# Order and engine of the weight splits in a linear-attention and mixture-of-experts kernel

## The chip, the cores and the metric

The kernel runs on one core of a Trainium2 chip. Its engines work side by side, each through its own list of instructions in order, and are tied together by semaphores: TensorE (PE), VectorE (DVE), ScalarE (ACT), GpSimd (POOL), and SyncE (SP), which issues most transfers. The metric is the device time in microseconds of one execution, as the median of several runs.

## What is computed

One transformer layer on 2048 tokens of width 512: `x = x + attention(layernorm(x))`, then `x = x + experts(layernorm(x))`. The reference, cut to what matters:

```python
# attention: 16 query heads, 4 key heads, width 128
q, k, v = x @ Wq.T, x @ Wk.T, x @ Wv.T          # q and k then rotated (rope)
qf, kf = elu(q) + 1.0, elu(k) + 1.0
def step(carry, inp):
    state, z = carry
    q_s, k_s, v_s = inp
    state = state + k_s[..., :, None] * v_s[..., None, :]
    z = z + k_s
    num = einsum('bhe,bhed->bhd', q_s, state)
    den = einsum('bhe,bhe->bh', q_s, z)[..., None] + EPS
    return ((state, z), num / den)
return out @ Wo.T
# experts: top 8 of 64 (32 real, 32 zero experts), gate, up and down projections
logits = xf @ w_cls.T
scores = softmax(logits)
act = silu(g) * u
y = einsum('eci,eih->ech', act, w_down)
```

## The kernel before

All data is float32. To keep precision on PE's faster float32 format, each operand is split in two: a high part, a copy rounded to that format (made on ACT), and a low part, the value minus its high part (a subtraction on DVE or POOL). A product is then three matmuls: high x high, high x low, low x high. Making high and low parts is most of what ACT, DVE and POOL do.

There are three blocks one behind the other, each closed by a barrier of all engines: `attention`, `routing` (projection by Wo, second layernorm, choice of experts, tables of slots) and `experts`. The change touches the first two.

`attention` goes over 16 chunks `c` of 128 tokens. A chunk has four groups `g` (one for each key head), and all engines loop over `n = 4 * c + g`. The loop is a software pipeline: PE projects group n, while rotation and feature map of n-1, the denominators of n-2, the transposes of n-3, the scores of n-4 and the output of n-5 are worked on. The order in which each engine takes them is written out by hand in its own loop. The 24 weight tiles of 128x512 (Wk, Wq, Wv) lie in `v_l` as loaded; `weight_high(i)` on ACT copies tile i to `w_h`, `weight_low(i)` on DVE writes `w_l`. PE's `project(u)` is a unit of twelve matmuls on four tiles; a chunk has six units, in the order k (0), q0 (1), q1 (2), v (3), q2 (4), q3 (5). In chunk 0 a unit also waits for its four low parts (line 206):

```python
if c == 0:
    eng.wait_ge(sm["wl"], 4 * i + 4)
```

So chunk 0 is where the splits and the pipeline's start share DVE and ACT. Before: ACT copies tiles 0 to 7 ahead of the loop, tiles 8 to 15 at n = 0 and 16 to 23 at n = 1, each batch at the head of its turn (lines 553 to 555). DVE makes tiles 8 to 11 at n = 0, 12 to 19 at n = 1 and 20 to 23 at n = 2, in a branch for chunk 0 that also holds the rotations (lines 433 to 444), ahead of `reduce` (denominators) and `feature_q` (which waits for ACT's `exps`).

Behind the last chunk the pipeline drains over n = 64 to 68. In its last three steps ACT and DVE also split tiles 0 to 5 of `wo` (`wo_high`, `wo_low`, lines 473 and 571), which lie in the same `v_l`, `w_h` and `w_l`. SP stores each group's output to `oT` in device memory (line 182) and loads the first three chunks of it again for routing (`load_o`).

`routing` also goes over 16 chunks. PE's `project(c, heads)` multiplies a chunk of oT by 16 tiles of Wo (one for each head, three matmuls each); in chunk 0 it waits for each head's `w_l` and for each quarter of `o_l` (lines 767 to 773). ACT (`high`, `o_high`) and DVE (`low`, `o_low`) split quarters 0 and 1 of o first, then tiles 6 and 7, quarter 2, tiles 8 and 9, quarter 3, and the tiles that are left. SP's `load(c)` brings the next chunk of oT and waits until it is stored.

## Time and profile before

| | us |
|---|---|
| median of 3 runs | 1025.86 |
| lowest and highest | 1021.43, 1032.84 |
| the profiled execution | 1021.43 |
| its span, first to last instruction | 1019.6 |
| attention block, about | 0 to 509 |
| routing block, about | 509 to 720 |

The profile holds one execution. The span leaves out 1.8 us around it. A row of a timeline begins with the start and the length of an instruction or of several of one kind in a row (xN), then engine, line of the program, operation, what it writes and reads; brackets at the end tell how long the engine had been idle and what released it. "PEclk" is the clock that TensorE was granted, 1.00 being 2.4 GHz and 0.50 being 1.2 GHz.

### The profile page before, as it was taken

What the parts mean: (1) busy time and instruction counts of PE and PEld (TensorE: products, weight loads), DVE (VectorE), ACT (ScalarE), POOL (GpSimd) and SP (SyncE); (2) the same over time, 40 slices, a digit from 0 to 9 for tenths busy, and PEclk for the clock granted to TensorE, in tenths of its full rate; (3) what the DMA queues carried; (4) which work ended last, traced back from release to release, by engine and by line L of the source; (5) the groups of instructions that cost most, each with busy time, mean ns of one, the idle gap of its engine ahead of it and who ended that gap; (6) DMA issues with size and microseconds to landing.
All of it is one profiled execution on the core that took longest, in us unless ns stands there. A gap on an engine that the chain in (4) does not pass through costs nothing. (4 is left out here: it accounts for less than half of the span.)

```text
span 1019.6 us, 14540 instructions
## 1 busy us (share of the span) xinstructions
PE 909.3 (89%) x4377; PEld 736.6 (72%) x4377; DVE 766.4 (75%) x1821; ACT 503.8 (49%) x867; POOL 494.5 (48%) x420
## 2 busy tenths in 40 slices
PE   4789999999999999999799999999759988697960
PEld 3577888888888888888578888888547666475850
DVE  6977988888888888888877777776577967586730
ACT  5454555555555555554652222222237867575730
POOL 2466766666667666666500000000046456667652
PEclk9999999999999999999999999999859999798995
DMA  8001111111111111112653653431149999898743
GB/s 296 6 32 47 58 37 58 47 58 42 51 54 46 48 48 58 42 48 86 262 193 133 257 194 127 142 136 65 64 149 286 330 287 269 227 276 262 216 64 41
DMA packets 52759, 131.03 MB, mean 129 GB/s; under 512 B 12156, under 2 KB 14588, under 8 KB 46528
## 3 DMA queue, kind: packets, MB, share of 16 engines
q1 hardware_dynamic: 41248, 114.67, 32.1%
q0 software_dynamic: 11424, 15.29, 8.3%
q8 instruction: 43, 0.70, 0.3%
q14 instruction: 44, 0.36, 0.1%
HBM read 106.53 MB, written 35.91 MB: 140 GB/s over the span
## 5 line engine op out<-in xcount | busy, mean ns | idle before, releaser
L595 POOL TENSOR_TENSOR a_t<-a_t 128x512 f32<-128x512 f32 x80 | 105.1, 1314 | 101.8 <-DVE a_t L358 101.8
L1076 DVE TENSOR_TENSOR w_l<-raw,w_h 128x1024 fp32r<-128x1024 f32 x96 | 114.8, 1222 | 13.4 <-ACT w_h L1069 11.7
L604 POOL TENSOR_TENSOR a_fQ<-a_fQ,a_den 128x512 f32<-128x512 f32 x64 | 88.0, 1376 | 71.8 <-DVE a_den L396 71.8
L213 PE MATMUL a_PQ<-w_h,a_xT_h 128*128 128x512 f32 x384 | 106.7, 400 | 10.3 <-DVE w_l L345 9.6
L775 PE MATMUL r_PY<-w_h,r_o_h 128*128 128x512 f32 x256 | 106.5, 416 | 3.4 <-DVE r_o_l L866 3.4
L1046 POOL TENSOR_SCALAR r_vr<-r_mv 128x1 f32<-128x1 f32 x16 | 8.4, 525 | 205.3 <-DVE r_mv L877 205.3
L1174 POOL DMA_INDIRECT out<-m_y,si x38 | 66.0, 1736 | 78.9 <-DMA out<-m_y,si 51.7
L213 PE MATMUL a_PQ<-w_l,a_xT_h 128*128 128x512 f32 x384 | 103.7, 392 | 0.0
L213 PE MATMUL a_PQ<-w_h,a_xT_l 128*128 128x512 f32 x384 | 103.5, 392 | 0.0
L775 PE MATMUL r_PY<-w_h,r_o_l 128*128 128x512 f32 x256 | 101.9, 398 | 0.0
L1069 ACT ACTIVATE w_h<-raw 128x1024 fp32r<-128x1024 f32 x96 | 97.8, 1054 | 8.1 <-DMA m_ident<-in_cr 7.8
L775 PE MATMUL r_PY<-w_l,r_o_h 128*128 128x512 f32 x256 | 101.7, 397 | 0.0
L392 DVE CUSTOM_DVE_ANT_0 a_m<-a_fQ,a_z 128x128 f32<-128x128 f32 x256 | 100.4, 445 | 0.0
L611 POOL TENSOR_TENSOR a_A_l<-a_A,a_A_h 128x512 fp32r<-128x512 f32 x64 | 89.0, 1390 | 6.5 <-ACT a_A_h L480 6.5
L213 PEld LDWEIGHTS a_PQ<-w_h,a_xT_h 128*128 128x128 f32 x384 | 70.2, 190 | 25.5 <-issue 11.4
L357 DVE TENSOR_TENSOR a_t<-a_PQ,a_tab 128x512 f32<-128x512 f32 x80 | 55.0, 688 | 42.0 <-PE a_PQ L213 42.0
L213 PEld LDWEIGHTS a_PQ<-w_l,a_xT_h 128*128 128x128 f32 x384 | 72.7, 189 | 15.7
L213 PEld LDWEIGHTS a_PQ<-w_h,a_xT_l 128*128 128x128 f32 x384 | 72.7, 189 | 15.3
L494 ACT ACTIVATE a_t<-a_t 128x512 f32<-128x512 f32 x80 | 50.0, 626 | 67.6 <-POOL a_t L595 67.6
L1155 POOL DMA_INDIRECT m_xg<-xn2d,si x58 | 71.9, 1239 | 19.9 <-issue 16.8
L480 ACT ACTIVATE a_QT_h<-a_PT 128x512 fp32r<-128x512 f32 x64 | 38.1, 596 | 80.9 <-PE a_PT L221 80.9
L775 PEld LDWEIGHTS r_PY<-w_h,r_o_h 128*128 128x128 f32 x256 | 48.7, 190 | 12.7 <-issue 3.8
(169 smaller groups left out, 2184.7 us busy)
## 6 DMA issues: line engine op xcount, KB each, us to landing
raw<-in_wgu SPq DMA_DIRECT2D x32, 1024.0 KB
oT<-a_o SPq DMA_DIRECT2D x64, 256.0 KB, 2.4
raw<-in_wd SPq DMA_DIRECT2D x32, 512.0 KB
...
```

The costliest lines, as they stand in the source:

```text
L213: last = eng.matmul(bank[:, :], a[:, k, :], w[:, 4 * i + k, :], start=s == 0 and k == 0, stop=s == 2 and k == 3)
L357: eng.tensor_tensor(heads(t1[:, r % 2, :]), q, spread(tab[:, c % 2, 0, :]), ALU.mult)
L392: last = eng.tensor_tensor_reduce(m[:, cols], fQ[:, n % 3, cols], z[:, c % 2, g * P:(g + 1) * P], 1.0, 1e-6, ALU.mult, ALU.add, den[:, n % ...
L494: eng.activation(t2[:, r % 2, :], t1[:, r % 2, :], ACT.Relu, scale=-1.0).then_inc(sm["r"], 1)
L595: eng.tensor_tensor(t1[:, r % 2, :], t1[:, r % 2, :], t2[:, r % 2, :], ALU.add).then_inc(sm["xr"], 1)
L604: eng.tensor_tensor(q, q, den[:, n % 2, :].unsqueeze(2).broadcast_to([P, 4, P]), ALU.mult).then_inc(sm["fs"], 1)
L611: eng.tensor_tensor(A_l[:, n % 2, :], A[:, n % 2, :], f(A_h[:, n % 2, :]), ALU.subtract).then_inc(sm["Al"], 1)
L775: last = eng.matmul(PY[c % 2][:, :], a[:, c % 2, h * P:(h + 1) * P], b[:, h, :], start=h == 0 and s == 0, stop=h == NH - 1 and s == 2)
L1069: eng.activation(high, src, ACT.Copy).then_inc(sm["m_wh"], 1)
L1076: eng.tensor_tensor(low, src, high.bitcast(F32), ALU.subtract).then_inc(sm["m_wl"], 1)
L1155: eng.indirect_dma_start(xg[:, e % 6, t, :], None, xn2d[:, :], bass.IndirectOffsetOnAxis(ap=ids[:, i:i + 1], axis=0), bounds_check=T - 1, ...
L1174: eng.indirect_dma_start(out[:, :], bass.IndirectOffsetOnAxis(ap=si[:, i:i + 1], axis=0), y[:, e % 4, t, :], None, compute_op=ALU.add).the ...
```

## The change

It changes three things. In chunk 0 of attention, ACT and DVE split four tiles at each of n = 0 to 3 (the tiles 4(g+2) to 4(g+2)+3). ACT does it at the head of each turn; DVE behind `reduce` and `feature_q` of the turn and, for n > 0, ahead of the rotation of q. The last tile of each four (11, 15, 19, 23) gets its low part on POOL, at the head of its turn, with a semaphore of its own (`wlp`), and PE waits for both. In the drain of attention, `wo_high` and `wo_low` are gone; all 16 tiles of Wo are split in routing: two tiles, then all of chunk 0 of o, then 14 tiles, and PE waits for the whole of `o_l` ahead of its first matmul. And SP waits at the end of attention until all of oT is stored, in place of routing's `load`.

```diff
+        def on_pool(i):
+            return i >= 11 and i % 4 == 3
...
                 load_o(2)
+                for b in range(2):
+                    eng.wait_ge(sm[f"oT{b}"], 16 * (NG // 2))
...
                     if c == 0:
-                        eng.wait_ge(sm["wl"], 4 * i + 4)
+                        eng.wait_ge(sm["wl"], 4 * i + 4 - max(i - 1, 0))
+                        if i >= 2:
+                            eng.wait_ge(sm["wlp"], i - 1)
...
                 for n in range(NG + 5):
                     c, g = divmod(n, 4)
-                    if c == 0:
-                        if g == 0:
-                            rotate(unit_k(0), rot_k(0), 0)
-                        if g == 2:
-                            v_low(0)
-                        for i in ((8,), (12,), (20,), ())[g]:
-                            for k in range(4):
-                                weight_low(i + k)
-                        rotate(unit_q(n), rot_q(n), 0)
-                        if g == 1:
-                            for k in range(4):
-                                weight_low(16 + k)
                     if 0 <= n - 2 < NG:
                         reduce(n - 2)
                     if 0 <= n - 1 < NG:
                         feature_q(n - 1)
                     if g == 2 and 1 <= c < NC:
                         s_low(c - 1)
-                    if g == 0 and 1 <= c < NC:
+                    if g == 0 and c < NC:
                         rotate(unit_k(c), rot_k(c), c)
-                    if g == 2 and 1 <= c < NC:
+                    if c == 0:
+                        for k in range(4):
+                            weight_low(4 * (g + 2) + k)
+                    if g == 2 and c < NC:
                         v_low(c)
-                    if 1 <= c < NC:
+                    if n < NG:
                         rotate(unit_q(n), rot_q(n), c)
...
-                    if n >= NG + 2:
-                        wo_low(2 * (n - NG - 2))
-                        wo_low(2 * (n - NG - 2) + 1)
...
-                    if n < 2:
-                        for i in range(8 + 8 * n, 16 + 8 * n):
-                            weight_high(i)
+                    if c == 0:
+                        for k in range(4):
+                            weight_high(4 * (g + 2) + k)
                     if 0 <= n - 1 < NG:
                         exps(rot_q(n - 1))
...
-                    if n >= NG + 2:
-                        wo_high(2 * (n - NG - 2))
-                        wo_high(2 * (n - NG - 2) + 1)
...
+                    if c == 0 and on_pool(4 * (g + 2) + 3):
+                        weight_low(4 * (g + 2) + 3)
                     if 0 <= n - 2 < NG:
                         scale(n - 2)
...
                 def load(c):
-                    eng.wait_ge(sm["r_ol"], 4 * (c - 2))
-                    for b in range(2):
-                        eng.wait_ge(sm[f"oT{b}"], 16 * (2 * c + 2))
+                    if c >= 3:
+                        eng.wait_ge(sm["r_ol"], 4 * (c - 2))
...
-                        if c >= 1:
-                            eng.wait_ge(sm["r_ol"], 4 * c + 4)
+                        eng.wait_ge(sm["r_ol"], 4 * c + 4)
...
                         if c == 0:
                             eng.wait_ge(sm["r_wol"], h + 1)
-                            eng.wait_ge(sm["r_ol"], h // 4 + 1)
```

ACT's list in chunk 0, before, from the high copies of tiles 8 to 11 to the first of q0's `exps` (`a_t` and `a_e` are the two activations of `exps`):

```order
L480 ACTIVATE w_h<-v_l 128x512 [waits e_st3]
L480 ACTIVATE w_h<-v_l 128x512 x3
L480 ACTIVATE w_h<-v_l 128x512 [waits e_st4]
L480 ACTIVATE w_h<-v_l 128x512 x3
L494 ACTIVATE a_t<-a_t 128x512 [waits e_xr]
L496 ACTIVATE a_e<-a_t 128x512 [waits e_r]
L480 ACTIVATE a_K_h<-a_fK 128x512 [waits e_f]
L480 ACTIVATE w_h<-v_l 128x512 [waits e_st5]
L480 ACTIVATE w_h<-v_l 128x512 x3
L480 ACTIVATE w_h<-v_l 128x512 [waits e_st6]
L480 ACTIVATE w_h<-v_l 128x512 x3
L494 ACTIVATE a_t<-a_t 128x512 [waits e_xr]
```

Only K's `exps` and high part stand among the copies. And now, from the high copies of tiles 12 to 15 on:

```order
L473 ACTIVATE w_h<-v_l 128x512 [waits e_st4]
L473 ACTIVATE w_h<-v_l 128x512 x3
L487 ACTIVATE a_t<-a_t 128x512 [waits e_xr]
L489 ACTIVATE a_e<-a_t 128x512 [waits e_r]
L473 ACTIVATE a_KT_h<-a_PT 128x512 [waits e_pt]
L473 ACTIVATE a_z<-a_PZ 128x512 [waits e_zc]
L473 ACTIVATE w_h<-v_l 128x512 [waits e_st5]
L473 ACTIVATE w_h<-v_l 128x512 x3
L487 ACTIVATE a_t<-a_t 128x512 [waits e_xr]
L489 ACTIVATE a_e<-a_t 128x512 [waits e_r]
L473 ACTIVATE a_V_h<-a_PQ 128x512 [waits e_pq]
L473 ACTIVATE a_xT_h<-a_PT 128x512 [waits e_pt]
L473 ACTIVATE w_h<-v_l 128x512 [waits e_st6]
```

The copies of tiles 12 to 15 (`e_st4`) stand behind K's exponentials and its high part, those of 16 to 19 (`e_st5`) behind q0's, and those of 20 to 23 (`e_st6`) behind the high part of the next x (`a_xT_h`).

DVE's list, before, from the low parts of tiles 12 to 15 to the low part of V:

```order
L345 TENSOR_TENSOR w_l<-v_l,w_h 128x512 [waits e_wh] x4
L357 TENSOR_TENSOR a_t<-a_PQ,a_tab 128x512 [waits e_f,e_pq]
L358 TENSOR_TENSOR a_t<-a_PQ,a_tab 128x512
L345 TENSOR_TENSOR w_l<-v_l,w_h 128x512 [waits e_wh] x4
L364 SCALAR_TENSOR_TENSOR a_fQ<-a_t,a_e 128x512 [waits e_e]
L401 TENSOR_TENSOR a_KT_l<-a_PT,a_KT_h 128x512 [waits e_th]
L333 TENSOR_SCALAR a_xn<-a_xin,a_mv,a_vr 128x512 [waits e_pt,e_rstd]
L379 TENSOR_TENSOR a_V_l<-a_PQ,a_V_h 128x512 [waits e_Vh]
```

Eight tiles and the rotation of q1 stand ahead of the first feature map of q. And now, from the low parts of tiles 8 to 10 to those of tiles 12 to 14 and the rotation of q1:

```order
L354 TENSOR_TENSOR w_l<-v_l,w_h 128x512 [waits e_wh] x3
L366 TENSOR_TENSOR a_t<-a_PQ,a_tab 128x512 [waits e_tab0,e_pq]
L367 TENSOR_TENSOR a_t<-a_PQ,a_tab 128x512
L373 SCALAR_TENSOR_TENSOR a_fK<-a_t,a_e 128x512 [waits e_e]
L332 BN_STATS a_st<-a_xin 128x6 [waits e_x1]
L334 BN_AGGR a_mv<-a_st 128x2 [waits e_bn]
L373 SCALAR_TENSOR_TENSOR a_fQ<-a_t,a_e 128x512 [waits e_e]
L354 TENSOR_TENSOR w_l<-v_l,w_h 128x512 [waits e_wh] x3
L366 TENSOR_TENSOR a_t<-a_PQ,a_tab 128x512 [waits e_f,e_pq]
L367 TENSOR_TENSOR a_t<-a_PQ,a_tab 128x512
```

The first feature map of q (`a_fQ`) stands now ahead of tiles 12 to 14; before, tiles 12 to 19 were ahead of it.

DVE's start of routing before, from the block's first operation on (`r_o_l` is the low part of a quarter of o, `w_l` of a tile of Wo):

```order
L937 MEMSET r_neg 128x1
L866 TENSOR_TENSOR r_o_l<-v_l,r_o_h 128x512 [waits e_r_oh] x2
L859 TENSOR_TENSOR w_l<-v_l,w_h 128x512 [waits e_r_woh] x2
L866 TENSOR_TENSOR r_o_l<-v_l,r_o_h 128x512 [waits e_r_oh]
L859 TENSOR_TENSOR w_l<-v_l,w_h 128x512 [waits e_r_woh] x2
L866 TENSOR_TENSOR r_o_l<-v_l,r_o_h 128x512 [waits e_r_oh]
L859 TENSOR_TENSOR w_l<-v_l,w_h 128x512 [waits e_r_woh] x6
```

Quarters of o and tiles of Wo took turns there. And now:

```order
L925 MEMSET r_neg 128x1
L847 TENSOR_TENSOR w_l<-v_l,w_h 128x512 [waits e_r_woh] x2
L854 TENSOR_TENSOR r_o_l<-v_l,r_o_h 128x512 [waits e_r_oh] x4
L847 TENSOR_TENSOR w_l<-v_l,w_h 128x512 [waits e_r_woh] x14
L933 CAST r_trib<-r_cst 128x128 [waits e_r_cst]
```

The four quarters now stand together behind two tiles, and 14 tiles follow.

## Rows read from the trace of the kernel before

**Rows 1.** The page: busy share of PE, and one group of POOL's instructions
```profile
PE 909.3 (89%) x4377; PEld 736.6 (72%) x4377; DVE 766.4 (75%) x1821; ACT 503.8 (49%) x867; POOL 494.5 (48%) x420
...
L595 POOL TENSOR_TENSOR a_t<-a_t 128x512 f32<-128x512 f32 x80 | 105.1, 1314 | 101.8 <-DVE a_t L358 101.8
```

**Rows 2.** Windows: stretch, us, busy PE, PEld, DVE, ACT, POOL, PEclk, DMA, GB/s
```profile
30.00:42.00 12.00, 8.44 (x40) 6.25 (x39) 11.97 (x26) 2.86 (x6) 3.25 (x3) 1.00 0.00 1
...
53.00:64.00 11.00, 8.33 (x37) 6.74 (x38) 10.04 (x29) 6.74 (x12) 7.82 (x8) 0.84 0.16 48
...
79.00:108.00 29.00, 27.37 (x130) 22.38 (x129) 22.52 (x57) 15.08 (x27) 18.05 (x16) 0.94 0.11 37
...
108.00:137.00 29.00, 29.00 (x147) 24.20 (x146) 24.89 (x66) 15.37 (x28) 19.12 (x17) 1.00 0.16 51
```

**Rows 3.** Waits of 0:50: who waited for whom, us, times, longest
```profile
PE a_PQ L213 <- DVE w_l L345: 9.6, 5, 3.4
```

**Rows 4.** Timeline of chunk 0 and the start of chunk 1
```profile
14.64 2.19 ACT L480 ACTIVATE w_h<-v_l 128x512 fp32r<-128x512 f32 x4 [0.84 <-DMA v_l<-in_wq]
...
18.14 3.58 DVE L345 TENSOR_TENSOR w_l<-v_l,w_h 128x512 fp32r<-128x512 f32 x4
...
18.30 1.66 POOL L595 TENSOR_TENSOR a_t<-a_t 128x512 f32<-128x512 f32 x1 [12.09 <-DVE a_t L358]
...
20.66 0.63 ACT L496 ACTIVATE a_e<-a_t 128x512 f32<-128x512 f32 x1
...
21.86 1.15 PE L213 MATMUL a_PQ<-w_h,a_xT_h 128*128 128x512 f32 x4 [2.20 <-DVE w_l L345]
...
23.76 1.08 PE L213 MATMUL a_PQ<-w_h,a_xT_l 128*128 128x512 f32 x4
...
28.24 1.17 PE L213 MATMUL a_PQ<-w_h,a_xT_h 128*128 128x512 f32 x4 [1.05 <-DVE w_l L345]
...
32.94 1.17 PE L213 MATMUL a_PQ<-w_h,a_xT_h 128*128 128x512 f32 x4 [1.70 <-DVE w_l L345]
...
36.42 0.60 ACT L480 ACTIVATE a_xT_h<-a_PT 128x512 fp32r<-128x512 f32 x1 [3.56 <-PE a_PT L221]
...
37.61 1.17 PE L213 MATMUL a_PQ<-w_h,a_xT_h 128*128 128x512 f32 x4 [1.22 <-DVE w_l L345]
...
42.20 1.09 PE L213 MATMUL a_PQ<-w_h,a_xT_h 128*128 128x512 f32 x4
...
46.48 0.29 DVE L392 CUSTOM_DVE_ANT_0 a_m<-a_fQ,a_z 128x128 f32<-128x128 f32 x1
...
57.29 0.50 PE L235 MATMUL a_PZ<-a_K_h,a_tri_r 128*128 128x512 f32 x1 [1.36 <-POOL a_K_l L599]
```

**Rows 5.** Timeline of the seam between attention and routing
```profile
500.78 1.14 ACT L480 ACTIVATE w_h<-v_l 128x512 fp32r<-128x512 f32 x2
...
503.32 0.68 DVE L414 TENSOR_TENSOR a_A<-a_PS,a_cst 128x512 f32<-128x512 f32 x1
...
507.92 0.60 ACT L480 ACTIVATE a_o<-a_PO 128x512 f32<-128x512 f32 x1 [0.69 <-PE a_PO L274]
...
508.96 0.38 SPq L162 DMA_DIRECT2D v_h<-oT  x1
...
509.76 1.15 ACT L989 ACTIVATE r_o_h<-v_l 128x512 fp32r<-128x512 f32 x2 [1.25 <-PEq L141]
...
511.26 0.47 PE L775 MATMUL r_PY<-w_h,r_o_h 128*128 128x512 f32 x1 [3.39 <-DVE r_o_l L866]
...
515.25 3.69 DVE L859 TENSOR_TENSOR w_l<-v_l,w_h 128x512 fp32r<-128x512 f32 x6
```

**Rows 6.** Windows with a low clock, columns as in rows 2
```profile
58.65:61.20 2.55, 2.55 (x11) 2.26 (x10) 2.55 (x5) 2.23 (x5) 2.55 (x3) 0.51 0.00 0
...
511.20:515.00 3.80, 3.74 (x10) 2.94 (x11) 3.80 (x7) 3.80 (x9) 0.00 (x0) 0.57 0.96 314
```

**Rows 7.** Tile a_o: its stores to oT, from issue to landing
```profile
DMA to landing us min/median/max: 2.3/2.4/5.3
```

More of the change, by code:

```diff
@@ L343, in weight_low @@
                 def weight_low(i):
+                    if on_pool(i):
+                        return
                     eng.wait_ge(sm["wh"], i + 1)
@@ L540, in out @@
                     copy(o[:, n % 2, :], PO[:, :], "o")
-                def wo_high(i):
-                    if i % 4 == 0:
-                        eng.wait_ge(sm[f"r_wo{i // 4}"], 16)
-                    copy(w_h[:, i, :], v_l[:, i, :], "r_woh")
                 weight_high(0)
@@ L591, in rstd, with weight_low @@
                     eng.tensor_tensor(vr[:, c % 2, 1:2], vr[:, c % 2, 0:1], neg[:, :], ALU.pow).then_inc(sm["rstd"], 1)
+                def weight_low(i):
+                    eng.wait_ge(sm["wh"], i + 1)
+                    eng.tensor_tensor(w_l[:, i, :], v_l[:, i, :], f(w_h[:, i, :]), ALU.subtract).then_inc(sm["wlp"], 1)
                 def add(u, r):
@@ L937, in _ @@
                 eng.memset(neg[:, :], -0.5).then_inc(sm["r_neg"], 1)
-                o_low(0, 0)
-                o_low(0, 1)
-                low(6)
-                low(7)
-                o_low(0, 2)
-                low(8)
-                low(9)
-                o_low(0, 3)
-                for i in range(10, NH):
+                low(0)
+                low(1)
+                for q in range(4):
+                    o_low(0, q)
+                for i in range(2, NH):
                     low(i)
@@ L994, in high, with o_high @@
                     copy(wo_h[:, i, :], v_l[:, i, :], "r_woh")
-                def o_high(c, quarters=range(4)):
+                def o_high(c):
                     if c >= NC:
@@ L1001, in o_high @@
                     eng.wait_ge(sm[f"r_o{c % 3}"], 16 * (c // 3 + 1))
-                    for q in quarters:
+                    for q in range(4):
                         rows, cols = quarter(c, q)
                         copy(heads(o_h[:, c % 2, cols]), rows, "r_oh")
-                o_high(0, (0, 1))
-                high(6)
-                high(7)
-                o_high(0, (2,))
-                high(8)
-                high(9)
-                o_high(0, (3,))
-                for i in range(10, NH):
+                high(0)
+                high(1)
+                o_high(0)
+                for i in range(2, NH):
                     high(i)
```

3 lines of the change are left out of this document (removed).

## Prediction

> **What bounds the kernel now.** First the page's busy line: TensorE (PE) is busy for 909.3 of 1019.6 us [rows 1]. Then the windows by stage: from 108 us on the attention loop keeps PE busy for 29.00 of 29.00 us at full clock, while 53:64 has 8.33 of 11 us with a granted clock of 0.84 and 79:108 has 27.37 of 29 with 0.94 [rows 2]. So a late start of the loop is not caught up later: PE has no slack to give. Then the waits of the first 50 us: PE waited 9.6 us, five times, for DVE's `w_l` [rows 3]; that is chunk 0, where the six weight blocks (units 0 to 5 of four 128-row tiles) are split while they are first used. Last the timelines of the two places that the change touches: chunk 0 [rows 4] and the seam between attention and routing [rows 5].
>
> **Part 1, chunk 0.** I follow the new order with the durations of before. Prices: four high copies on ACT take 2.19 us, the two activations of `exps` 0.63 each with a small gap, 1.3 together; four low parts on DVE take 3.58 beside a POOL operation; a unit on PE runs from 21.86 to 24.84, 2.98 [rows 4]; a POOL operation on 128x512 takes 1.31 [rows 1], up to 1.66 beside DVE's `w_l` [rows 4]. Without POOL six low parts take 3.69, 0.61 each [rows 5].
> Unit 2 (needs tiles 8 to 11). ACT is through tile 11 at 16.83, as before. POOL does tile 11 at 16.9 to 18.2, just ahead of the first rotation's addition, which started at 18.30 and still does. DVE does three tiles from 18.14: 2.9 in place of 3.58. Unit 2 starts at 21.2, 0.7 sooner than 21.86.
> Unit 3 (tiles 12 to 15). Before, ACT copied these high halves ahead of `exps(k)`, in time that it idled. Now they stand behind `k_high`, and `exps(q0)` behind them; and DVE has `feature_q(0)`, which needs `exps(q0)`, ahead of its low parts. So: `k_high` done 23.6, four copies 25.7, `exps(q0)` 27.0, `feature_q(0)` 27.7, three low parts at 0.61 and an end 29.5. Unit 3 starts at 29.6 against 28.24: +1.4.
> Unit 4 (16 to 19). The rotation of q1 (two operations at 0.6 apart and an end, 1.3) to 30.8; POOL's addition, behind its tile 15, to 32.2; `exps(q1)` 33.5; `feature_q(1)` 34.2; three low parts, partly beside POOL's tile 19 and its scaling, 36.3. Beside the same wait stand `turn_low_k`, `normal(1)` and `reduce(0)`, some 2.4 us of DVE in a wait of 2.8, which cost nothing. Unit 4 starts at 36.4 against 32.94: +3.5.
> Unit 5 (20 to 23) is the worst. Its high copies stand behind `xT_high(1)`, which waits for the transpose of the next x, and that stands on PE behind unit 4. Before, ACT had long made them and then idled 3.56 us before `xT_high(1)` at 36.42 [rows 4]. Now: unit 4 ends 39.4 (40.4 with the clock, below), transpose and `xT_high(1)` 41.7, four copies 43.9, `exps(q2)` 45.2, `feature_q(2)` 45.9, three low parts beside POOL 48.1. Unit 5 starts at 48.2 against 37.61: +10.6.
> The clock. After PE had done little from 54 to 58 us its granted clock was 0.51 over 58.65:61.20, and after the seam 0.57 over 511.20:515.00 [rows 6]: the 1.2 GHz level for about 2.5 and 3.7 us, half of which is lost. In the new order PE idles 3.9 us ahead of unit 4 and some 7 ahead of unit 5, so I add 1.0 to unit 4 (may or may not fall) and 2.1 to unit 5. The bounds are 0 and 2.5 for each, the upper the half of a fall of 5 us.
> Unit 5 then ends at 53.3, q0's transpose and `rest_k` about 1.1 later, and unit 6 starts at 54.4 against 42.20. That is +12.2 on PE, but before the delay passed on was DVE's: `reduce(2)` started at 46.48, 4.3 us after unit 6. Now rotation q3, `turn_low_q(0)` and `stats(2)` end at 56.0, so DVE is +9.5. The chain to `sum_k(1)` (57.29 before, after a wait for `K_l` [rows 4]) is DVE, ACT and POOL work of the same kinds; with fewer hold-ups in it I take +8.7 there. PE's stalls up to that point in before (much of the 2.67 idle us of 53:64) are swallowed. The low clock right behind, 1.25 us, is likely gone too, since PE now arrives there out of a busy stretch: +7.5. From there on the two kernels do the same in the same state, and I let the stalls of 79:108 return. Bounds of the start: +4 (no low clock and a cheaper chain) and +11 (5 us of it at both units).
>
> **A rule weighed.** Beside POOL's addition four low parts took 3.58 us, and with POOL idle six took 3.69 [rows 4, 5]. The Trainium skill's GPSIMD Engine Reference (Architecture) says that POOL shares its SBUF interfaces with VectorE and contends with its instructions that read two SBUF tensors; a low part is one. By that rule, and the trace agrees, a tile moved to POOL returns up to 1.1 us of the DVE time it saves if low parts run beside it. This is why I book almost no gain for the four moved tiles (0.7 on unit 2 alone). Were there no contention, DVE would gain 0.6 for each.
> The low clock after a quiet PE is the row's [rows 6]. The Trainium skill's TensorE: Matmul & The Clock Gate (Part 1) says that the array stands at half rate by default and activity releases it; by the rule unit 5 starts slow, as I have it, and without it the sum would be 2 to 3 us less.
>
> **Part 2, the seam.** Six of `wo`'s tiles are no longer split in the last three steps of attention. There two high copies stood ahead of the output copy at 500.78, two low parts (1.96 us) held `masked(63)` until 503.32, and two more copies of both kinds followed; the last output copy ran 507.92 to 508.52 [rows 5]. Without them the mask starts two low parts (1.2) sooner, at 502.1, and ends at 502.8; `A_h` 503.5, `A_l` on POOL 504.9, the last `attend` 506.1, output copy 506.7. That is 1.8 sooner.
> SP then waits for the stores of `oT` before the block ends. A store lands 2.4 us after its issue [rows 7]: 506.8 + 2.4 = 509.2, and 0.4 for the barrier (before, SP's last issue ended at 509.34 and ACT started at 509.76 [rows 5]) gives 509.6. All engines wait here, but the 1.8 pays for it: -0.1. Bounds: -1.3 (landing hidden) and +3 (the maximum of 5.3 [rows 7]).
> Then routing. Before, PE started 1.50 us after ACT, at 511.26, since six heads were ready and each quarter of o was waited for by itself. Now ACT does two high copies and four of `o_h`, 6 at 0.55 = 3.3, the last `o_low` ends 0.75 later, and PE starts 4.05 after ACT: +2.55. Behind it nothing falls short: a matmul takes 0.24 (eight between 21.86 and 23.76 [rows 4]), so a head takes PE 0.71 and its low part DVE 0.61. ACT and DVE have six tiles more before `o_high(1)` and `o_low(1)`, which end about 525.8, while PE comes to chunk 1 at 526.6: hidden by 0.8 us, and a later price if that cover goes. PE has been idle 7 us in place of 3.4, so 0.4 more of the low clock. `load(c)` loses only waits that are met, at no cost. Seam: -0.1 + 2.55 + 0.4 = +2.9.
> Experts are untouched.
>
> **Sum.** +7.5 + 2.9 = +10.4. The profiled execution took 1021.43, so 1031.8 for it; the median of the runs is 1025.86, 4.4 above it, so 1036.3 for a median.
>
> **Rivals.** (A) Not slower: DVE, and no order, bounds chunk 0. It is busy 11.97 of the 12 us of 30:42 [rows 2], and four low parts fewer save it 3.6. Then the start is -3.6, the seam +2.9, 1025.2. For it: that busy share. Against it: much of it is low parts done early, and the new order puts an ACT chain ahead of them. It decides at `feature_q(0)`: DVE must find `exps(q0)` done there, and ACT cannot have it before 27.0. (B) Given back: a fresh start also removes the stalls of 79:108 (1.6 idle and about 1.4 of clock [rows 2]): +7.4, 1033.3. For it: those stalls are remnants of a late DVE. Against it: `sum_k(1)` brings both kernels to the same state. (C) More clock and contention: low clock for 5 us at units 4 and 5 and behind `sum_k(1)` (+1.9 and +1.3) and the longer landing (+1): +14.6, 1040.5. Speaks for it: the idle stretches are longer than any of before.
>
> **How the numbers follow.** My forecast 0.48, A 0.10, B 0.25, C 0.17. The forecast's own range is 1032 to 1040. With the other cases the range is 1028 to 1042: A and the tail of C are left out. A measurement tells about 1% (10.3 us) from no change, that is 1036.1. C (0.17), half of my forecast (0.24) and a little of B (0.04) lie above: 0.45. Faster by over 1% would need more than A and gets 0.03; the rest, 0.52, lies within.
>
> **What would show it.** Right: unit 2 a little earlier, then PE waiting at units 3, 4, 5 with starts near 29.6, 36.4 and 48; ACT's copies of tiles 20 to 23 after `xT_high(1)`; full PE from about 115 on; the attention's last output copy 1.8 sooner relative to the loop, the barrier as late as before, PE's first routing matmul 4 us after ACT's. Wrong: `exps(q0)` ahead of 27 us, unit 5 before 44, or PE's idle of chunks 1 and 2 gone.

## The result, and the profile after

The changed kernel took 1045.31 us (median of 6 runs, 1041.33 to 1047.62), the kernel before on the same chip 1028.0 (6 runs, 1021.43 to 1032.84). The ratio is 1.0155, with a 95% interval of 1.0121 to 1.0190: slower by 12 to 20 us. This ratio, like those below, is the recorded one of fast runs and not the quotient of the two medians, which would be 1.0168 (all 20 runs of the changed kernel on record have a median of 1043.3). The forecast was +10.4, and its range of 1028 to 1042 does not hold 1045.31. The profiled execution took 1039.17, its span is 1037.4 with a mean granted clock of 0.943 (before 1019.6 and 0.957).

The page shows the same work (914.7 us of PE where [rows 1] has 909.3) and one large new wait:

```profile
PE 914.7 (88%) x4377; PEld 741.6 (71%) x4377; DVE 767.0 (74%) x1817; ACT 502.9 (48%) x867; POOL 496.6 (48%) x424
...
L220 PE MATMUL a_PQ<-w_h,a_xT_h 128*128 128x512 f32 x384 | 109.3, 407 | 21.8 <-DVE w_l L354 21.8
```

PE now waits 21.8 us for low parts where it waited 9.6 [rows 3]: the damage is in chunk 0. The windows (columns as in rows 2) say what kind of time it is:

```profile
30.00:42.00 12.00, 6.79 (x23) 5.14 (x22) 8.27 (x18) 1.75 (x3) 4.10 (x3) 0.72 0.00 1
53.00:64.00 11.00, 11.00 (x49) 8.97 (x49) 8.00 (x20) 2.18 (x4) 3.96 (x4) 0.90 0.04 12
37.80:42.30 4.50, 4.50 (x12) 3.55 (x13) 0.50 (x1) 0.00 (x0) 0.00 (x0) 0.59 0.00 0
50.40:56.30 5.90, 5.89 (x18) 4.73 (x19) 0.67 (x2) 0.23 (x1) 0.00 (x0) 0.60 0.01 3
91.00:120.00 29.00, 27.39 (x131) 22.38 (x130) 22.51 (x58) 15.97 (x28) 17.84 (x15) 0.94 0.12 41
120.00:149.00 29.00, 29.00 (x147) 24.22 (x146) 24.85 (x65) 15.35 (x29) 19.36 (x16) 1.00 0.15 46
527.20:531.00 3.80, 3.76 (x9) 2.99 (x10) 3.80 (x7) 3.80 (x8) 0.00 (x0) 0.50 0.80 283
```

First line: DVE, busy for 11.97 of these 12 us in before [rows 2], is busy for 8.27. Nothing is saturated there; the engines wait for each other. Lines 3 and 4 are units 4 and 5, both at about the 1.2 GHz level. Line 5 is the window 79:108 of [rows 2], 12 us later and with the same 27.4 busy us and the same clock of 0.94; from there on PE is full (line 6), but for one wait of 0.9 us between chunks 9 and 10. The timeline of chunk 0, against [rows 4]:

```profile
20.95 1.99 PE L220 MATMUL a_PQ<-w_h,a_xT_h 128*128 128x512 f32 x4 [2.66 <-DVE w_l L354]
25.95 0.63 ACT L489 ACTIVATE a_e<-a_t 128x512 f32<-128x512 f32 x1
26.61 1.06 DVE L373 SCALAR_TENSOR_TENSOR a_fQ<-a_t,a_e 128x512 f32<-128x512 f32 x1 [2.32 <-ACT a_e L489]
27.60 1.88 DVE L354 TENSOR_TENSOR w_l<-v_l,w_h 128x512 fp32r<-128x512 f32 x3
29.58 1.17 PE L220 MATMUL a_PQ<-w_h,a_xT_h 128*128 128x512 f32 x4 [3.15 <-DVE w_l L354]
30.76 1.29 POOL L584 TENSOR_TENSOR a_t<-a_t 128x512 f32<-128x512 f32 x1 [3.63 <-DVE a_t L367]
31.20 1.13 DVE L340 TENSOR_SCALAR a_xn<-a_xin,a_mv,a_vr 128x512 f32<-128x512 f32 x1
32.01 1.45 POOL L580 TENSOR_TENSOR w_l<-v_l,w_h 128x512 fp32r<-128x512 f32 x1
32.25 1.36 DVE L401 CUSTOM_DVE_ANT_0 a_m<-a_fQ,a_z 128x128 f32<-128x128 f32 x1
32.75 0.63 ACT L489 ACTIVATE a_e<-a_t 128x512 f32<-128x512 f32 x1
34.39 0.66 DVE L373 SCALAR_TENSOR_TENSOR a_fQ<-a_t,a_e 128x512 f32<-128x512 f32 x1
34.97 2.73 DVE L354 TENSOR_TENSOR w_l<-v_l,w_h 128x512 fp32r<-128x512 f32 x3
37.80 2.04 PE L220 MATMUL a_PQ<-w_h,a_xT_h 128*128 128x512 f32 x4 [5.21 <-DVE w_l L354]
43.00 0.60 ACT L473 ACTIVATE a_xT_h<-a_PT 128x512 fp32r<-128x512 f32 x1 [9.13 <-PE a_PT L228]
43.49 2.18 ACT L473 ACTIVATE w_h<-v_l 128x512 fp32r<-128x512 f32 x4
46.22 0.63 ACT L489 ACTIVATE a_e<-a_t 128x512 f32<-128x512 f32 x1
47.58 2.73 DVE L354 TENSOR_TENSOR w_l<-v_l,w_h 128x512 fp32r<-128x512 f32 x3
50.41 2.05 PE L220 MATMUL a_PQ<-w_h,a_xT_h 128*128 128x512 f32 x4 [7.45 <-DVE w_l L354]
56.33 1.09 PE L220 MATMUL a_PQ<-w_h,a_xT_h 128*128 128x512 f32 x4
69.96 0.50 PE L242 MATMUL a_PZ<-a_K_h,a_tri_r 128*128 128x512 f32 x1 [1.35 <-POOL a_K_l L588]
```

Units 2 to 6 start at 20.95, 29.58, 37.80, 50.41 and 56.33. Read it upwards from unit 5: its low parts (47.58) stand behind a feature map, that behind `exps` (46.22), that behind the copies of 43.49, those behind `a_xT_h`, and that waits for PE's own unit 4. The seam, against [rows 5]:

```profile
518.13 0.60 ACT L473 ACTIVATE a_o<-a_PO 128x512 f32<-128x512 f32 x1 [1.79 <-PE a_PO L281]
519.17 0.38 SPq L165 DMA_DIRECT2D v_h<-oT  x1
522.81 0.33 SPq L722 DMA_DIRECT2D r_cst<-in_cr  x1
522.82 1.15 ACT L973 ACTIVATE w_h<-v_l 128x512 fp32r<-128x512 f32 x2 [4.10 <-PEq L144]
527.24 0.79 PE L763 MATMUL r_PY<-w_h,r_o_h 128*128 128x512 f32 x1 [9.15 <-DVE r_o_l L854]
```

The barrier opens at 522.8, 4.7 us behind the start of the last output copy (in before 1.8), and PE's first routing matmul starts 4.4 behind ACT (1.5).

**One table for all kernels.** Marks in us from each span's start: units 4 and 5; the first sum over keys of chunk 1 (`a_PZ<-a_K_h,a_tri_r`), here "chunk 1"; the start of the last output copy; SP's first issue in routing (barrier); PE's first routing matmul; DVE's last step of routing (writes `r_L`); then the rest of the span, the experts. The median of before on the same chip was 1028.0 beside after, 1024.44 beside e1 to e4, 1026.66 beside e5, e6, e7 and e10, and 1024.35 beside the others.

| kernel | unit 4 | unit 5 | chunk 1 | copy | barrier | PE | `r_L` | experts | median | ratio (95%) |
|---|---|---|---|---|---|---|---|---|---|---|
| before | 32.9 | 37.6 | 57.3 | 507.9 | 509.7 | 511.3 | 744.9 | 274.7 | | |
| after | 37.8 | 50.4 | 70.0 | 518.1 | 522.8 | 527.2 | 761.9 | 275.5 | 1045.31 | 1.0155 (1.0121, 1.0190) |
| e1_chunk0 | 37.8 | 51.4 | 70.6 | 523.0 | 524.9 | 526.4 | 761.0 | 276.4 | 1041.03 | 1.0160 (1.0123, 1.0197) |
| e2_seam | 32.6 | 37.2 | 56.9 | 503.7 | 508.3 | 512.7 | 746.8 | 279.7 | 1027.43 | 1.0025 (1.0003, 1.0048) |
| e3_actorder | 32.6 | 39.8 | 61.1 | 512.8 | 514.7 | 516.2 | 749.6 | 276.2 | 1029.45 | 1.0059 (1.0031, 1.0088) |
| e4_dveorder | 39.9 | 53.3 | 72.1 | 519.5 | 521.3 | 522.8 | 756.4 | 287.0 | 1038.95 | 1.0122 (1.0078, 1.0165) |
| e5_pool | 32.3 | 42.6 | 64.7 | 513.4 | 515.3 | 516.8 | 749.8 | 279.0 | 1032.43 | 1.0091 (1.0057, 1.0125) |
| e6_spwait | 32.7 | 37.3 | 57.0 | 507.6 | 512.3 | 513.9 | 747.8 | 278.9 | 1028.21 | 1.0015 (0.9985, 1.0044) |
| e7_warm | 37.9 | 48.9 | 66.2 | 512.8 | 517.4 | 521.8 | 755.3 | 283.8 | 1039.0 | 1.0160 (1.0086, 1.0234) |
| e8_seam_nowait | 32.6 | 37.3 | 57.0 | 502.3 | 504.1 | 508.5 | 742.3 | 283.8 | 1027.12 | 1.0036 (1.0006, 1.0067) |
| e10_lowfirst | 34.3 | 42.9 | 62.5 | 510.7 | 515.5 | 519.9 | 754.5 | 282.2 | 1040.12 | 1.0172 (1.0106, 1.0238) |
| e11_wait_load | 32.7 | 37.4 | 57.0 | 507.6 | 511.4 | 512.9 | 747.4 | 279.3 | 1027.7 | 1.0045 (1.0015, 1.0075) |
| e12_drain | 32.5 | 37.1 | 56.8 | 505.7 | 507.9 | 509.4 | 743.7 | 278.9 | 1025.09 | 1.0021 (0.9997, 1.0045) |
| e13_drain_pool2 | 30.8 | 35.4 | 55.1 | 502.3 | 504.5 | 506.0 | 738.9 | 278.7 | 1021.58 | 0.9990 (0.9957, 1.0023) |

The marks tell more than the medians, but three things have to be known of them. First, the experts stage, whose instructions no edit touches, takes 274.7 to 287.0 us, mean 279.6; before's own profile has the shortest. Second, six kernels have before's chunk 0 unchanged (before, e2, e6, e8, e11, e12), and their marks lie at 32.5 to 32.9 for unit 4 and at 56.8 to 57.3 for chunk 1, before's own profile latest each time: a difference under 0.5 us there says nothing. Third, two stretches of low clock in chunks 1 and 2 come or stay away. From the mark of chunk 1 to that of chunk 2 PE stands still for 1.6 us in every kernel, but the interval is 30.3 to 30.6 us where the mean granted clock is 0.94 or 0.95, 28.9 where it is 1.00, and 33.35 in e3_actorder, where it is 0.86. From chunk 2 to 3 PE never stands still, and the interval is 31.2 us at a clock of 0.945 and 29.6 at 1.00. Two of these stretches, in before (chunk 2 to 3) and in e3_actorder (chunk 1 to 2), columns as in rows 2:

```profile
88.50:91.90 3.40, 3.40 (x13) 2.83 (x11) 3.40 (x6) 1.83 (x3) 3.33 (x4) 0.51 0.00 0
```

```profile
61.00:70.50 9.50, 9.45 (x30) 8.09 (x31) 7.36 (x18) 4.38 (x8) 6.18 (x6) 0.50 0.21 55
```

Why a stretch comes in one kernel and not in another stays open: e2 and e8 differ only behind the attention loop, and e2 has 30.33 us where e8 has 28.92. So a difference of 1.6 us (or twice that) in `r_L` is explained only once these two intervals are looked at.

### The profile page after: what moved, and what is told of

It reads as the page before. It is cut to its first block and busy times, and to the rows that moved or that the text cites. A ratio compares the mean times of both kernels' runs of the same rounds, so it can differ in the third digit from the quotient of the medians.

```text
span 1037.4 us, 14514 instructions
## 1 busy us (share of the span) xinstructions
PE 914.7 (88%) x4377; PEld 741.6 (71%) x4377; DVE 767.0 (74%) x1817; ACT 502.9 (48%) x867; POOL 496.6 (48%) x424
## 5 line engine op out<-in xcount | busy, mean ns | idle before, releaser
L220 PE MATMUL a_PQ<-w_h,a_xT_h 128*128 128x512 f32 x384 | 109.3, 407 | 21.8 <-DVE w_l L354 21.8
L1056 DVE TENSOR_TENSOR w_l<-raw,w_h 128x1024 fp32r<-128x1024 f32 x96 | 114.7, 1222 | 14.6 <-ACT w_h L1049 13.0
L220 PE MATMUL a_PQ<-w_l,a_xT_h 128*128 128x512 f32 x384 | 105.9, 399 | 0.0
L763 PEld LDWEIGHTS r_PY<-w_h,r_o_h 128*128 128x128 f32 x256 | 48.9, 191 | 18.6 <-DVE r_o_l L854 9.6
## 6 DMA issues: line engine op xcount, KB each, us to landing
v_l<-in_wq SPq DMA_DIRECT2D x4, 1024.0 KB, 12.5
```

What stands on the lines that cost most here:

```text
L220: last = eng.matmul(bank[:, :], a[:, k, :], w[:, 4 * i + k, :], start=s == 0 and k == 0, stop=s == 2 and k == 3)
L763: last = eng.matmul(PY[c % 2][:, :], a[:, c % 2, h * P:(h + 1) * P], b[:, h, :], start=h == 0 and s == 0, stop=h == NH - 1 and s == 2)
L1056: eng.tensor_tensor(low, src, high.bitcast(F32), ALU.subtract).then_inc(sm["m_wl"], 1)
```

## The experiments

**Each part alone.** e1_chunk0 takes chunk 0's part of the change and leaves drain, wait and routing as before:

```diff
+        def on_pool(i):
+            return i >= 11 and i % 4 == 3
...
+                    if c == 0:
+                        for k in range(4):
+                            weight_low(4 * (g + 2) + k)
...
+                    if c == 0:
+                        for k in range(4):
+                            weight_high(4 * (g + 2) + k)
```

> Only the chunk 0 part of the change (new order on ACT and DVE, four low parts on POOL), seam as before. Theory (order in chunk 0): the profiled change has its first routing-side delays on top of a loop that is 11 to 12 us late, so +11 to +12.5 us against before, unit 5 of chunk 0 at about 50.4 us. Rival (the seam is the larger part): +5 us or less here.

Measured: chunk 1 at 70.6 (+13.3), `r_L` +16.1, ratio 1.016 (+12.6 to +20.2 us), unit 5 at 51.4. That is more than the +11 to +12.5 expected, and the rival (+5 or less) is out. By the ratio the whole loss is chunk 0's, but the interval is 7.6 us wide and leaves room for a seam of about 4. e2_seam takes the rest of the change alone:

```diff
-                    if n >= NG + 2:
-                        wo_low(2 * (n - NG - 2))
-                        wo_low(2 * (n - NG - 2) + 1)
...
+                for b in range(2):
+                    eng.wait_ge(sm[f"oT{b}"], 16 * (NG // 2))
```

> Only the seam part (no wo splits in attention's drain, all 16 in routing, PE waits for all of o_l, SP waits for the stores), chunk 0 as before. Theory: last output copy 2.0 us sooner, SP's wait +2.9, PE's start in routing +2.9, low clock behind it +1: together +4.9 us. Rival (seam pays for itself, as the recorded sum nearly had it with +2.9): +3 us or less.

Measured: `r_L` +2.0. Against its own chunk 1 and with what its two intervals lack counted back (1.8), the last output copy is 2.0 sooner, the barrier 2.8 later behind that copy, PE 2.9 later behind ACT: about +4, nearer to the theory (+4.9) than to the rival (+3 or less). The ratio is 1.0025 (+0.3 to +4.9 us) and does not tell the two apart.

**Chunk 0 taken apart.** The three edits in it, each by itself on the kernel before. ACT's order:

```diff
-                    if n < 2:
-                        for i in range(8 + 8 * n, 16 + 8 * n):
-                            weight_high(i)
+                    if c == 0:
+                        for k in range(4):
+                            weight_high(4 * (g + 2) + k)
```

> Before, with only ACT's order in chunk 0 changed (four high copies at each of n = 0 to 3). Theory A (DVE's order does it: feature_q ahead of the low parts): here DVE still makes tiles 12 to 19 ahead of feature_q(0), so units 3 and 4 start no later, unit 5 waits for the copies behind the next x's high part, about 38 us against 37.6: 0 to +1.5 us. Theory B (ACT's order does it, by tiles 20 to 23 behind xT_high): +6 us or more.

Measured: units 3 and 4 no later than before (27.9, 32.6), unit 5 at 39.8 (+2.2) because the copies of tiles 20 to 23 now start at 36.55, behind `a_xT_h`, and DVE idles 2.53 us for them; chunk 1 +3.8, then the 9.5 us of low clock shown above (+2.8 in that interval) and the next one missing (-1.6), so `r_L` +4.7, ratio 1.006 (+3.2 to +9.0 us). Neither theory had this: the places are A's, with units 3 and 4 on time and unit 5 late, but the price lies between A's (0 to +1.5) and B's (+6 or more). DVE's order alone:

```diff
                     if 0 <= n - 2 < NG:
                         reduce(n - 2)
                     if 0 <= n - 1 < NG:
                         feature_q(n - 1)
...
+                    if c == 0:
+                        for k in range(4):
+                            weight_low(4 * (g + 2) + k)
```

> Before, with only DVE's order in chunk 0 changed (reduce and feature_q ahead of the turn's four low parts), all low parts on DVE, ACT as before. Theory A (DVE's order does it): feature_q(0) waits for exps(q0), which ACT has only at 29.6 us behind tiles 16 to 23, so unit 3 at 33, unit 4 at 40, unit 5 at about 50 us: +10 to +13 us. Theory B (ACT's order does it): +3 us or less.

Measured: chunk 1 +14.8, `r_L` +11.5 (both low-clock stretches absent, 3.2 us), ratio 1.012, as theory A had it; unit 5 came at 53.3, later than the 50 expected. DVE's timeline in e4_dveorder shows the mechanism at its first occurrence:

```profile
28.80 0.69 DVE L364 SCALAR_TENSOR_TENSOR a_fQ<-a_t,a_e 128x512 f32<-128x512 f32 x1 [5.21 <-ACT a_e L487]
29.41 2.49 DVE L345 TENSOR_TENSOR w_l<-v_l,w_h 128x512 fp32r<-128x512 f32 x4
32.05 2.04 PE L213 MATMUL a_PQ<-w_h,a_xT_h 128*128 128x512 f32 x4 [5.45 <-DVE w_l L345]
```

DVE stands 5.21 us in front of a feature map for which ACT has no exponentials yet (eight high copies are ahead of them in ACT's old order), while the low parts of unit 3, which it could make, stand behind; PE waits 5.45. With ACT's new order beside it both waits are shorter (after: 2.32 and 3.15), which fits that the whole of chunk 0's part costs less at chunk 1 (e1, 13.3) than the two orders by themselves (14.8 and 3.8). POOL's tiles alone:

```diff
+        def on_pool(i):
+            return i >= 11 and i % 4 == 3
...
+                    if c == 0 and on_pool(4 * (g + 2) + 3):
+                        weight_low(4 * (g + 2) + 3)
```

> Before, with only the four low parts (tiles 11, 15, 19, 23) moved from DVE to the heads of POOL's turns. Theory of POOL's order: tile 23 stands on POOL behind scale(0) and the addition of q2, so unit 5 starts at about 41 us in place of 37.6: +2 to +4 us. Rival (relief of DVE, the bound of chunk 0): -2 to -4 us.

Measured: unit 4 at 32.3 (0.2 to 0.6 sooner than in the six kernels with before's chunk 0), unit 5 at 42.6 (5.0 later, where about 41 was expected), chunk 1 +7.4, `r_L` +4.9 (both low-clock stretches absent, and 1.2 us new between chunks 9 and 10), ratio 1.009 (+5.9 to +12.8 us). The rival, that relief of DVE gains 2 to 4 us, is out. POOL and PE in e5_pool:

```profile
38.60 1.40 POOL L615 TENSOR_TENSOR a_fQ<-a_fQ,a_den 128x512 f32<-128x512 f32 x1 [6.94 <-DVE a_den L403]
39.96 1.25 POOL L606 TENSOR_TENSOR a_t<-a_t 128x512 f32<-128x512 f32 x1
41.18 1.26 POOL L602 TENSOR_TENSOR w_l<-v_l,w_h 128x512 fp32r<-128x512 f32 x1
42.59 2.04 PE L218 MATMUL a_PQ<-w_h,a_xT_h 128*128 128x512 f32 x4 [6.84 <-POOL w_l L602]
```

Tile 23 stands at the head of POOL's fourth turn, behind the third turn's scaling and addition; POOL idled 6.94 us before them and could have made it. PE has stood still for 6.84 us when that one tile comes, and then runs at the low clock (4 matmuls in 2.04 where full speed takes 1.17).

**Counter-test.** e10_lowfirst is the whole change with DVE's low parts at n = 1 to 3 ahead of `reduce` and `feature_q` again:

```diff
+                    if 1 <= n < 4:
+                        for k in range(4):
+                            weight_low(4 * (g + 2) + k)
                     if 0 <= n - 2 < NG:
                         reduce(n - 2)
...
-                    if c == 0:
+                    if n == 0:
                         for k in range(4):
-                            weight_low(4 * (g + 2) + k)
+                            weight_low(8 + k)
```

> The changed kernel with one thing put back: on DVE the turn's low parts stand ahead of reduce and feature_q for n = 1 to 3 (still three on DVE and one on POOL; ACT and the seam as changed). Theory (DVE's low parts behind feature_q are the cause): unit 3 of chunk 0 at 27.7 us in place of 29.6, unit 4 at 33 in place of 37.8, unit 5 at 40.5 in place of 50.4, so 8 to 10 us less than the changed kernel, +6 to +8 against before. Rival (POOL's part and contention are the cause): no more than 3 us less than the changed kernel.

Measured: units 3 to 5 at 28.0, 34.3 and 42.9, chunk 1 at 62.5, 7.4 sooner than after, `r_L` 7.4 sooner: a little under the 8 to 10 of the theory, far over the 3 of the rival. DVE's order inside the turn is worth 7.4 of the 12.7 us at chunk 1; the 5.2 left are ACT's order and POOL's tiles, which e3 and e5 price at 3.8 and 7.4 alone. Its median shows none of this gain (ratio 1.0172, 4 runs, an interval 1.3% wide; experts 282.2 in its profile). The marks of one profile each carry this verdict, not the time.

**The clock.** e7_warm is the whole change with extra matmuls ahead of units 2 to 5 (8, 10, 16 and 24, into a bank that is overwritten later), so that PE does not stand still:

```diff
+                    if c == 0:
+                        for k in range((0, 0, 8, 10, 16, 24)[i]):
+                            eng.matmul(PO[:, :], xT_h[:, 0, k % 4, :], w_h[:, k % 4, :], start=True, stop=True)
```

> The changed kernel with 8, 10, 16 and 24 extra matmuls on PE (into a bank that nobody reads yet) ahead of units 2 to 5 of chunk 0, in time that it idles, to keep its clock up. They compute nothing that is used. Theory (the low clock is a part of the delay, about 2.5 us at each of units 4 and 5): those units take 3 us in place of 4.6 and 5, unit 6 starts 4 to 5 us sooner than 56.3, and the time is 4 us less than the changed kernel. Rival (the clock is not on the path): within 1.5 us of the changed kernel.

Measured, unit 5 in e7_warm:

```profile
48.86 1.16 PE L223 MATMUL a_PQ<-w_h,a_xT_h 128*128 128x512 f32 x4 [2.03 <-issue]
```

Four matmuls in 1.16 where after has 2.05. Units 4 and 5 with what hangs on them take 2.84 and 3.73 (37.91 to 40.75, 48.86 to 52.59); in after 4.56 and 5.92. The low clock so costs 1.7 and 2.2. Unit 4 starts at 37.9, where after has 37.8; unit 5 starts 1.5 sooner, since unit 4 ends sooner, and unit 6 and chunk 1 come 3.75 us sooner than in after, a little under the 4 to 5 expected. The time does not show it (ratio 1.016, 4 runs, an interval 1.5% wide).

**The seam taken apart.** e6_spwait is before with SP's wait behind its 1 MB load of `oT`, e11_wait_load with the wait ahead of it (in this order):

```diff
                 load_o(2)
+                for b in range(2):
+                    eng.wait_ge(sm[f"oT{b}"], 16 * (NG // 2))
...
+                for b in range(2):
+                    eng.wait_ge(sm[f"oT{b}"], 16 * (NG // 2))
                 load_o(2)
```

> Before, with only SP's wait for all stores of oT at the end of attention. Theory (landing is exposed): the barrier opens 2.8 us later behind the last output copy than before (4.7 in place of 1.8 us), all of it on the path: +2.8 to +3.5 us. Rival (the wait is hidden by the rest of the barrier, as the recorded lower bound had it): +0.5 us or less.

> The kernel before, with SP's wait for the stores put AHEAD of load_o(2) (the 1 MB load), not behind it. In e6 (wait behind the load) the barrier opened 4.7 us after the start of the last output copy, a landing of some 3.7 us, where the median landing over the attention loop is 2.4. Theory 1 (the store waits for shares of the DMA queues with the load issued just behind it): the store lands in 2.3 to 2.5 us here, the barrier opens 3.7 to 4.0 us after the start of the last output copy, and ACT and DVE then wait for the load, whose issue is now later by 2.5 to 3 us, unless it had time to spare. Rival (3.7 us is what the last landing and its notice cost with no later store behind it, whatever stands in the queues): the barrier opens 4.6 to 4.8 us after that start, as in e6. Time of either 1.000 to 1.004.

SP's timeline around it, first e6_spwait, then e11_wait_load:

```profile
508.60 0.38 SPq L162 DMA_DIRECT2D v_h<-oT  x1
...
512.34 0.33 SPq L734 DMA_DIRECT2D r_cst<-in_cr  x1
```

```profile
510.66 0.32 SPq L162 DMA_DIRECT2D v_h<-oT  x1
...
511.39 0.33 SPq L734 DMA_DIRECT2D r_cst<-in_cr  x1
```

In both the last output copy starts at 507.6, and the store is issued right behind it at about 508.2. Ahead of the load the wait is met at 510.6, a landing of 2.3 us; behind the load SP waits 2.9 us from 509.0 on, to 511.9, a landing of 3.7. The barrier opens 3.8 against 4.8 us behind the start of the copy. That is the first theory: the load issued behind the store slows its landing. All 14 profiles agree: the last store lands in 3.4 to 3.7 us in the 13 kernels that issue the load behind it, whether anything waits for it or not, and in 2.3 in e11 alone. It could be read in before already (DMA issues of 508.4 to 510, with KB and us to landing):

```profile
oT<-a_o SPq DMA_DIRECT2D x1, 256.0 KB, 3.5
```

The landing is not hidden: `r_L` is 2.9 us later in e6 and 2.5 in e11. Both kernels are within 0.8% of before, and the intervals do not say which is faster.

e8_seam_nowait is e2 without the wait, routing's loads keeping their own:

```diff
-                for b in range(2):
-                    eng.wait_ge(sm[f"oT{b}"], 16 * (NG // 2))
```

> The kernel before with the seam part of the change alone, without SP's wait for the stores at the end of the attention block (the loads of routing keep their own waits, as before). In e2 (with the wait) the seam part gave: last output copy -2.0 us against sum_k(1), barrier 4.6 us behind the start of that copy, PE's first routing matmul 4.4 us behind ACT's first, experts' mark +1.9 in all. Theory (three independent terms, drain -2.0, wait +2.8, PE's start +2.9): here the wait's term is gone, so the barrier opens 1.8 us behind the start of the last output copy as in before, PE still starts 4.4 behind ACT, first routing chunk about +0.6, and the mark that ends routing stands, against sum_k(1), +1.3 to +1.8 of before. Rival (routing's first transfers set PE's start, and the earlier barrier only uncovers them): PE starts 6 us or more behind ACT, and the mark stands as in e2 against sum_k(1). Time of the first 1.001 of before, of the second 1.003.

Measured: barrier 1.8 behind the copy, PE 4.4 behind ACT, the copy at 502.3. Its `r_L` is 2.6 us sooner than before's, but it lacks both low-clock stretches (3.25 together by the intervals); against chunk 1 and with them counted it stands at +1.0, where +1.3 to +1.8 was expected. The terms of the seam so add up (-2.1 + 2.9 + 0.2), and only the clock's part was smaller (its first chunk of routing took 13.1 us, before's 13.0, after's 14.1).

**Towards a better kernel.** e12_drain keeps wo's six tiles in the drain but `wo_high` behind the output copy of its step, and `wo_low` from one step later on, behind the mask:

```diff
+                    if n >= NG + 2:
+                        for i in ((0, 1), (2, 3, 4), (5,))[n - NG - 2]:
+                            wo_high(i)
...
+                    if n >= NG + 3:
+                        for i in ((0, 1, 2, 3, 4), (5,))[n - NG - 3]:
+                            wo_low(i)
```

> The kernel before with the same work, but in the last three steps of attention ACT's output copy stands ahead of the high copies of wo (2, 3 and 1 tiles in the three steps) and DVE's low parts stand behind the masks (5 and 1 tiles in the last two steps). No wait at the block's end, the start of routing as before. Theory: the drain's gain of the change (last output copy 2.0 us sooner against sum_k(1)) comes from the order, not from leaving the tiles out, so it is had here with PE's start 1.5 us behind ACT kept: last output copy -1.8, barrier -1.0 to -1.8, mark that ends routing -1.0 to -1.8, time 0.998 to 0.999 of before. Rival (the tiles' work, wherever it stands, ends behind the last output copy and holds the barrier): the barrier opens as late as in before or later, mark 0 to +1, time 1.000.

Measured against its own chunk 1: copy 1.7 sooner, barrier and PE 1.4 sooner, `r_L` 0.6 sooner, where at least 1.0 was expected; its first chunk of routing took 13.8 us where before's took 13.0 (granted clock 0.50 over its first 4 us and 0.86 over the next 4, where before has 0.57 and 1.00), so the clock ate half. The drain's gain is thus one of order and needs no tile left out, but it is too small to be timed: ratio 1.0021 (0.9997 to 1.0045). e13_drain_pool2 adds tiles 11 and 15 on POOL:

```diff
+        def on_pool(i):
+            return i in (11, 15)
```

> e12 and, in chunk 0, the low parts of tiles 11 and 15 alone on POOL, with the orders of DVE and ACT as before. e5 (tiles 11, 15, 19 and 23 on POOL) started unit 4 0.6 us sooner and then unit 5 5 us later, which is where tiles 19 and 23 stand behind POOL's scaling and additions. Theory (the late unit 5 comes from tiles 19 and 23 alone): unit 4 at 32.2 to 32.6, unit 5 at 36.6 to 37.2, sum_k(1) 0.3 to 1 us sooner than in e12, the mark that ends routing 0.3 to 1 sooner. Rival (POOL's work for any tile delays its additions of the rotations and gives DVE back what it saved): units 3 to 5 no sooner than in before, sum_k(1) 0 to +3 us.

```profile
15.88 1.31 POOL L602 TENSOR_TENSOR w_l<-v_l,w_h 128x512 fp32r<-128x512 f32 x1 [9.88 <-ACT w_h L487]
...
25.75 1.34 POOL L602 TENSOR_TENSOR w_l<-v_l,w_h 128x512 fp32r<-128x512 f32 x1
...
30.76 1.17 PE L218 MATMUL a_PQ<-w_h,a_xT_h 128*128 128x512 f32 x4 [0.54 <-issue]
```

Both tiles fall into time in which POOL was idle. Units 3 to 5 start at 27.2, 30.8 and 35.4, against 27.8, 32.5 and 37.1 in e12; chunk 1 is 1.7 us sooner, more than expected. How much of it is the edit's is open: unit 1 already starts 1.0 us sooner (15.28 against 16.27), ahead of any edited instruction that PE waits for, because the matmuls of unit 0 went from one in 0.46 to one in 0.23 us at about 14.0 us where e12's did so at about 16.0. The profile's granted clock is 1.00 over 11 to 17 us in both and does not show this. What stands is that tiles 11 and 15 don't hold PE up and that tile 23 does. `r_L` is 6.0 us sooner than before's, 1.6 of it an absent low-clock stretch; the median of 1021.58 is the lowest of all, and the ratio, 0.9990 (0.9957 to 1.0023), no proven gain.

## Why the prediction was wrong

The mechanism and nearly every place were right. Several sizes were short, nearly all on the same side, and they add up to the miss: `r_L` came +17.0 late where +10.4 was booked. Of these 6.6 us about 4.0 arose up to chunk 1, 1.2 between chunks 9 and 10 and 1.9 at the seam, less 0.4 for a low-clock stretch that gave back more than booked.

**Chunk 0, right.** Unit 2 at 21.2 (measured 20.95), unit 3 at 29.6 (29.58), `exps(q0)` done at 27.0 (26.6), `exps(q1)` done at 33.5 (33.4); the copies of tiles 20 to 23 behind `xT_high(1)`; unit 5 the worst. From the end of unit 4 to unit 5 7.8 us were booked and 8.1 measured.

**Chunk 0, the failed step: "`turn_low_k`, `normal(1)` and `reduce(0)`, some 2.4 us of DVE in a wait of 2.8, which cost nothing".** They took 3.8 (30.60 to 34.39 in the timeline above) and ended 1.0 us behind `exps(q1)`. Two of the operations met POOL: `normal(1)` ran 1.13 us beside an addition on POOL (0.53 without), and the first operation of `reduce(0)` 1.36 us beside POOL's own low part, which ended at 33.46 (0.28 for each of the following three). The three low parts behind them took 2.73, not 2.1. I had weighed contention for the low parts alone and used it to book no gain; it also had a price for the other operations. The Trainium skill's SBUF — State Buffer (SBUF: two separate sides) calls the pair of ports that both engines share an exclusive lock, on which the loser blocks until the other's whole instruction is over. The trace agrees in kind: the two slowed operations end only 0.28 and 0.15 us behind POOL's, which is less than their own 0.53 and 0.28, so it does not show that they stood still for the whole of it (POOL's spans are rough in the profile). So unit 4 started at 37.8, not 36.4.

**The clock, sized short.** "I add 1.0 to unit 4 (may or may not fall) and 2.1 to unit 5": by e7_warm it is 1.7 and 2.2. The fall came at unit 4 as it did at unit 5, and I had halved it for want of a row. Unit 6 came at 56.33, not 54.4: 1.4 from unit 4's start, 0.5 from its length (4.5 for the 4.0 booked), 0.3 from the way to unit 5, less 0.3 between units 5 and 6.

**"with fewer hold-ups in it I take +8.7 there".** `reduce(2)` started at 58.27, +11.8 where +9.5 was booked, and from it to chunk 1 the chain took 11.7 us where before had 10.8. The 0.9 that came on top is one feature map, which waited 0.3 us for ACT and then ran 1.37 beside POOL's scaling, where before's ran 0.69:

```profile
59.50 1.04 POOL L593 TENSOR_TENSOR a_fQ<-a_fQ,a_den 128x512 f32<-128x512 f32 x1 [1.21 <-DVE a_den L405]
59.72 1.37 DVE L373 SCALAR_TENSOR_TENSOR a_fQ<-a_t,a_e 128x512 f32<-128x512 f32 x1 [0.30 <-ACT a_e L489]
```

From there to chunk 1 both kernels take the same 9.0 us (61.01 to 69.96; 48.32 to 57.29 in before), so there were no hold-ups to take out. Chunk 1 came +12.7. This discount had no row behind it, and it is the largest error of one step (1.7 us: 0.8 taken off, 0.9 that came on top).

**The start of the loop.** "The low clock right behind, 1.25 us, is likely gone too": it was gone (28.93 us from chunk 1 to 2, before 30.54), which gave back 1.6. But it is gone in e8 too, which has before's chunk 0, and it is there in e1, which has the new one. So it was luck, and the reason given for it is not shown; with it `r_L` would have come +18.6. The 1.2 us that came on top later (30.71 us from chunk 9 to 10) were in no step. At full clock PE waits 0.9 us there for POOL's low part of K, and the interval is this long in all five kernels with four tiles on POOL and in none of the other nine; why, stays open.

**The seam.** Drain -1.8: measured -2.0, right. "A store lands 2.4 us after its issue": 3.6 here, since the 1 MB load is issued behind it (e6, e11). It was within the stated bounds, which had the maximum of 5.3 for it, but the value taken was the median of a row in which nearly all stores have no large load behind them; before's own last store, which has it, took 3.5. PE's start +2.55: +2.9. Low clock +0.4: the first chunk of routing took 1.1 more (527.20:531.00 above has 0.50). Sum +4.8, booked +2.9.

**The last part of the miss** is in the base. 4.4 us lay between the profile of before and its median, and 6.1 between those of after. That lies likely in the experts stage: 274.7 and 275.5 us in these two profiles, 279.6 over fourteen; the runs without a profile do not tell. So the miss of 9.0 us (1045.31 for 1036.3) is 6.6 at `r_L`, 0.8 in the experts and 1.7 in this step from profile to median. And 1045.31 was measured beside a 1028.0 for before; by the ratio the change is +15.9 on the 1025.86 of the forecast, 1041.8, with an interval from 1038.3 to 1045.4, whose middle lies just inside the range of 1028 to 1042.

**The rivals.** (A) DVE bounds chunk 0: false. DVE's busy share fell from 11.97 to 8.27 of 12 us while the time grew. The test named for it, whether DVE finds `exps(q0)` done, showed 2.32 us of idle; and e5, which only relieves DVE, is slower. (B) The stalls of 79:108 go: false for this kernel, the window 91:120 has them to 0.02 us (the clock's part, 1.6 us, does go in e2, e3, e4, e5, e7, e8 and e13). (C) More clock and contention and a longer landing: this was the right one in its direction, +14.6 for the sum against +17.0 at `r_L`. Contention and landing were its terms; its clock term behind chunk 1 did not come. It had a chance of 0.17. Two of its terms were no matter of chance: the landing behind a load stood in before's own trace (3.5 us), and so did operations of DVE that run twice as long beside POOL's (the feature map at 43.81 took 1.32 us in before, the one at 47.72 0.69).
